# Conditioning parts regrouped over four attention rounds, and one batch routed a round sooner, in an attention and expert kernel

## The reference

```
x = x + attention(cond(x, side, side, w1, u1, time))
x = x + experts(cond(x, side, side, w2, u2, time))
```

## Time and profile before

| | us |
|---|---|
| three runs, median (lowest to highest) | 524.43 (522.4 to 524.53) |
| the profiled execution, its time | 527.21 |
| the profiled execution, its span | 525.4 |
| PE busy in the span | 456.2 (87%) |
| DVE busy | 345.7 (66%) |
| ACT busy | 310.5 (59%) |
| POOL busy | 213.5 (41%) |

### The profile page before, as it was taken

The page is one execution under the profiler, slowest core; times in us unless marked ns, Lnnn a source line. Parts: engine busy times, 40 slices in busy tenths (PEclk is TensorE's granted clock), DMA queues, the critical chain, the costliest instruction groups (busy, mean ns, idle before and its releaser), DMA issues.

```text
span 525.4 us, 10372 instructions
## 1 busy us (share of the span) xinstructions
PE 456.2 (87%) x3073; PEld 343.8 (65%) x3073; DVE 345.7 (66%) x1204; ACT 310.5 (59%) x854; POOL 213.5 (41%) x224
## 2 busy tenths in 40 slices
PE   4487889999999889998998957868999999999476
PEld 1266677787777768786886643446777777777222
DVE  4948769559668678739859883835567777674043
ACT  4366687689585787968798670113436656666200
POOL 0323402006012365111357877403666666666600
PEclk9889899999999999999999977979999999999879
DMA  7931494000030011200029997499855555560297
GB/s 268 418 138 36 87 193 108 20 1 1 0 83 0 30 65 71 78 5 2 21 82 380 406 408 282 116 300 310 276 143 161 157 148 156 166 166 18 55 404 293
DMA packets 47318, 79.49 MB, mean 151 GB/s; under 512 B 8266, under 2 KB 31127, under 8 KB 46880
## 3 DMA queue, kind: packets, MB, share of 16 engines
q1 hardware_dynamic: 36544, 55.08, 33.4%
q0 software_dynamic: 7680, 16.93, 8.9%
q10 hardware_dynamic: 3040, 6.82, 4.0%
HBM read 56.54 MB, written 26.44 MB: 158 GB/s over the span
## 4 chain that ended last, share of the span: by engine, by line
PE 52%; DVE 15%; ACT 14%; DMA 9%; issue 5%; POOL 3%; SPq 2%; DVEq 0%; POOLq 0%; ACTq 0%
PE ps L1698 11%; PE ps L1400 8%; PE ps L1719 7%; PE ps L1525 6%; ACT lg L696 4%; DVE lg L1042 3%; ACT lg L639 3%; DMA pairs<-pair_rows 3%; PE ps L1448 2%; PE ps L1396 2%; POOL slot_rows L618 2%; PE ps L1397 2%; PE ps L1398 2%; DMA xrow<-slot_rows 2%; DMA pair_rows<-eout,dest 2%
## 5 line engine op out<-in xcount | busy, mean ns | idle before, releaser
L625 POOL DMA_INDIRECT pair_rows<-eout,dest x93 | 91.9, 988 | 62.4 <-ACT eout L639 40.4
L696 ACT ACTIVATE lg<-lg,mneg 128x128 f32<-128x128 f32 (+1 forms) x128 | 56.4, 443 | 26.1 <-DVE mneg L1042 26.1
L1698 PE MATMUL ps<-wts,xg 128*64 (+1 forms) x512 | 70.2, 339 | 1.2 <-DVE xg L1319 1.1
L546 POOL DMA_INDIRECT slot_rows<-rows,pair_slot x48 | 48.4, 1009 | 34.6 <-issue 23.6
L1698 PEld LDWEIGHTS ps<-wts,xg 128*64 128x64 f32 x512 | 52.3, 141 | 13.2 <-issue 5.7
L1525 PE MATMUL ps<-oT,wo_sb 128*128 128x256 f32 x240 | 54.4, 380 | 0.0
L1319 DVE COPY xg<-ps 128x512 f32<-128x512 f32 (+1 forms) x50 | 33.4, 667 | 31.0 <-PE ps L1400 28.8
L1525 PEld LDWEIGHTS ps<-oT,wo_sb 128*128 128x128 f32 x240 | 44.6, 190 | 6.2 <-ACT oT L639 0.7
L838 ACT ACTIVATE sact<-ps 128x192 f32<-128x192 f32 (+1 forms) x50 | 16.2, 325 | 51.5 <-PE ps L1698 49.1
L639 ACT ACTIVATE lg<-lg,rinv 128x128 f32<-128x128 f32 (+1 forms) x128 | 45.9, 449 | 0.8 <-DVE rinv L1050 0.8
L1719 PE MATMUL ps<-wts,aT 96*64 96x256 f32 (+1 forms) x256 | 46.0, 379 | 0.4 <-ACT aT L639 0.4
(11 more groups left out here) (237 smaller groups left out, 1199.8 us busy)
## 6 DMA issues: line engine op xcount, KB each, us to landing
wts<-in_experts_dram SPq DMA_DIRECT2D x22, 640.0 KB, 14.0
xrow<-slot_rows SPq DMA_DIRECT2D x188, 65.0 KB
pairs<-pair_rows SPq DMA_DIRECT2D x16, 512.0 KB, 9.6
wts<-in_experts_dram ACTq DMA_DIRECT2D x10, 640.0 KB, 7.9
slot_rows<-zero SPq DMA_DIRECT2D x1, 4160.0 KB, 24.3
wT<-in_wq_t_dram SPq DMA_DIRECT2D x4, 512.0 KB, 6.2
wq_raw<-in_wq_l_dram SPq DMA_DIRECT2D x1, 2048.0 KB, 14.7
wo_sb<-in_wo_l_dram SPq DMA_DIRECT2D x1, 2048.0 KB, 20.6
```

The costliest lines, as they stand in the source:

```text
L546: nc.gpsimd.indirect_dma_start(out=slot_d, out_offset=bass.IndirectOffsetOnAxis(ap=pair_slot[:, t, k:k + 1], axis=0), in_=r[:, k, :], in_o ...
L625: nc.gpsimd.indirect_dma_start(out=pair_d, out_offset=bass.IndirectOffsetOnAxis(ap=dest[:, d:d + 1], axis=0), in_=out_rows(d), in_offset=N ...
L696: ins = nc.scalar.activation(t, t, ACT.Exp, bias=mneg[:, u % 2, c:c + 1], scale=-1.0, accum_out=rsum[:, u % 2, c:c + 1])
L1698: ins = nc.tensor.matmul(ps[h * R:(h + 1) * R, 2 + u % 2, k * I2:(k + 1) * I2], xg[u % len(xg)][:, k, cc, h * R:(h + 1) * R], moving, star ...
```

## The change

Four rounds (5, 6, 10 and 11) do three parts where they did two, the second of the late ones being new; all parts behind come sooner, and rounds 13 and 14 have none. Batch 1 is routed from round 8 on instead of 9, and its two blocks are sent in rounds 10 and 11 instead of 11 and 12. The sends of block 4, which stood in two halves around the last `cond_sums` on POOL, stand together.

```
+        THICK = (5, 6, 10, 11)
+
         def round_parts(u):
-
-            return round_jobs[2 * u:2 * u + 1], round_jobs[2 * u + 1:2 * u + 2]
-
-
-        routed_from = (4, 9, 12)
-        block_round = (6, 7, 11, 12, 13, 14)
+            first = 2 * u + sum(1 for r in THICK if r < u)
+            return round_jobs[first:first + 1], round_jobs[first + 1:first + (3 if u in THICK else 2)]
+
+
+        routed_from = (4, 8, 12)
+        block_round = (6, 7, 10, 11, 13, 14)
...
                         if part == 2:
-                            for t in sent_in(u):
-                                if t == TB * QUICK:
-                                    number_rows(t)
-                                    send_rows(t, range(TOPK // 2))
                             cond_sums((c, jb))
...
                 for t in sent_in(u):
-                    if t == TB * QUICK:
-                        send_rows(t, range(TOPK // 2, TOPK))
-                    else:
-                        number_rows(t)
-                        if t == LAST[0] - 1:
-                            number_last_rows(LAST[1])
-                        send_rows(t, range(TOPK))
+                    number_rows(t)
+                    if t == LAST[0] - 1:
+                        number_last_rows(LAST[1])
+                    send_rows(t, range(TOPK))
```

## The result

The change made the kernel slower: 542.44 us median of four runs (540.51 to 547.41) against 524.48 of before on the same chip (522.4 to 525.1), ratio 1.0356, 95% interval 1.0311 to 1.04. On another chip six more runs gave 540.38 (e9), ratio 1.033 [1.0273, 1.0387]; the median of all ten is 540.8, 16.4 over the 524.4 of before's fifteen. I had forecast 537.3.

A forecast was written before the change was run, and what follows sets the result against it. The prediction took PE, busy 456 of 525 us, and its chain of waits through the attention rounds as the bound. Waits +9.8, port +1.6 and clock +1.5 made +12.9, giving a median of 537.3 us, range 527.5 to 543.

The forecast's parts named there:

- PE idle, rounds 6 to 15, without the added port: PE's waits in rounds 6 to 15, summed round by round: 20.05 us after against 10.3 before, +9.8.
- port, beyond what before had: POOL's additions slow DVE at the pick in round 5 (0.6) and the hits of round 11 (1.0): +1.6 us.
- clock: PE at half clock behind new waits of 5.75 and 4.1 us, most of it at round 6: +1.5 us.
- two stretches of 1.95: Upper limit of the clock cost: 1.95 us twice, behind the new waits of 5.75 and 4.1 us.
- rounds 13 to 15, 1.6 us of idle: Rounds 13 to 15 lose their parts; PE's idle time of 2.75 us becomes about 1.6.
- my 5.75: Round 6: part 2 ahead of the pick makes it 4.06 us later; PE's idle 1.7 becomes 5.75 us.
- upper bound of 5.1: Port: both POOL additions met in full in rounds 5 and 11, 2.55 us each, 5.1 in all.
- the 0.9 for the gate logits: Round 12 with the start of 13: part 3 ahead of the next logits makes route_logits another 0.9 us late.
- A: Rival: only round 6's stall is real, later rounds absorb each other's lateness; +3.7, 528 us; chance 0.19.
- B: Rival: faster through the freed tail, rounds 13 to 15 emptied and round 6's stall shrunk; -4.5, 520 us; chance 0.05.
- C: Rival: evens out within 0.5%, round 6's loss paid by rounds 7 and 14; 525 us; chance 0.08.
- D: Rival: POOL's additions met in full at both places, both stretches at 1.2 GHz; +17.9, 542 us; chance 0.08.

The follow-up runs named there:

- e9: The changed kernel once more, unaltered, on another chip: 540.38 us, ratio 1.033 to before.
- e6: The changed kernel with POOL's two additions held back until the pick of batch 0 (round 5) and the hits of block 3 (round 11) are through: 539.63 us.
- e5: The changed kernel with unread matmuls on PE ahead of two waits, 7 in round 6 and 6 in round 12: 535.3 us, ratio 1.0242 to before.
- e1: The kernel before with single part (0,3,2) moved from the front of round 6 to round 5, ahead of the pick of batch 0: 530.86 us.
- e4: The changed kernel with part (1,3,2) moved from late in round 11 to early in round 12: 535.22 us, ratio 1.0222 to before.
- e10: The changed kernel with picks ahead of the late parts and part (1,3,2) in round 12 instead of 11: 532.75 us, ratio 1.0146 to before.
- e7: The kernel before with part 1 of jobs (0,3) and (1,2) moved from late to early in rounds 5 and 10: 518.38 us, ratio 0.9894.
- e12: The kernel before with the eight sends of block 4 together behind POOL's two additions of job (1,3): 528.72 us, ratio 1.0082.
- e2: The kernel before with the picks of batches 0 and 1 ahead of the late part of their round: 523.93 us, ratio 0.9999.
- e8: The kernel of e7 with ACT's copy hh of batch 3 behind the filled rows of round 7: 519.47 us, ratio 0.9918 to before.
- e3: The changed kernel with the picks of batches 0 and 1 ahead of the late parts of their rounds: 539.07 us, ratio 1.0303 to before.
- e11: The changed kernel with a new table of parts, and ACT's early exponentials and hh behind fill_rows: 531.83 us, ratio 1.0145 to before.

## Why the prediction was wrong in size and right in kind

**The sum.** I forecast +12.9 on the profiled execution and found +13.3, but by accident: the start and the tail gave back 4.2 us of the 17.5 lost in the rounds. The steps, one by one:

| step | forecast | measured |
|---|---|---|
| PE idle, rounds 6 to 15, without the added port | +9.8 | +9.5 |
| port, beyond what before had | +1.6 | +2.6 (e6) |
| clock | +1.5 | +4.8 (after against e5) |
| not assigned | | +0.6 |
| together | +12.9 | +17.5 in the rounds |

The rows say what the lost time consists of, not what each would give back: with POOL's work moved (e6) the waits fell by 3.3 us, rounds 6 and 12 by 1.75.

**The step that failed is "I take +1.5" for the clock.** I bounded it by two stretches of 1.95 and reasoned that PE would be the path in round 6 only. The two stretches cost 3.1, and the third, 1.7, I had not counted at all, because I looked only at the two long waits: round 15's wait of 2.3 us was forecast as part of "rounds 13 to 15, 1.6 us of idle". That the clock falls behind a wait of this length was open from the rows of before, where 1.7 kept it and 3.42 did not; I took the upper row as if it were the limit. The trace of before had more, in round 0, which the prediction did not use: there 0.50 follows a wait of 1.59 us, 3.9 us behind another of 2.72.

```profile
55.31 1.04 PE L1400 MATMUL ps<-ident,lg 128*128 128x128 f32 x4 [1.59 <-DVE mneg L1042]
```

```profile
55.38:58.79 3.41, 3.41 (x17) 3.41 (x18) 3.38 (x2) 0.60 (x1) 2.90 (x3) 0.50 0.00 0
```

**The port** was taken at 1.6 over what before had. e6 shows 3.3 in the two waits; of the 1.7 in round 6 about 0.7 was in my 5.75 already, since the pick of before also ran beside POOL, beside its masks (0.59 below and 0.81 in the earlier trace rows against 0.23 and 0.48 in e6), so that the added part is 1.0 and 1.6, 2.6 in all, half of the upper bound of 5.1. DVE, then POOL, in before:

```profile
156.86 0.59 DVE L1075 TENSOR_SCALAR picked<-rrep 128x128 f32<-128x128 f32 x1
```

```profile
156.73 1.22 POOL L519 TENSOR_SCALAR_AFFINE_SELECT bm<-bm 128x512 f32<-128x512 f32 x2 [10.24 <-DMA bm<-bias_rows]
```

The wait of round 12 has the rest, in two hits of block 3 in the changed kernel:

```profile
270.80 0.91 DVE L1102 SCALAR_TENSOR_TENSOR hit<-key,ktop,rcomb 128x64 f32<-128x64 f32 x1
...
271.64 1.29 DVE L1102 SCALAR_TENSOR_TENSOR hit<-key,ktop,rcomb 128x64 f32<-128x64 f32 x1
...
272.87 0.28 DVE L1102 SCALAR_TENSOR_TENSOR hit<-key,ktop,rcomb 128x64 f32<-128x64 f32 x1
```

The first two end at 271.71 and 272.93, with POOL's two additions (271.63 and 272.85), and in e6 a `rsum` of four columns, 0.16 us elsewhere, took 1.11 until one of them ended. So DVE's operation ended only with POOL's. This agrees with the rule of the Trainium skill (SBUF — State Buffer, Who interferes with whom), that the later one is held for the other's length. The sum stayed under the bound because each pair of additions began beside operations that went on at their usual lengths: 0.7 us in round 5, beside the `MAX8` and the replacements of the pick, 0.4 in round 11, beside the addition to x. The time of the held operation itself passes inside the wait, too.

**Waits, place by place** (forecast, measured): round 6 5.75 and 0.6 of port, 6.7; round 7 with the start of 8 0.95, 0.8; round 8 1.25, 1.8; round 9 0.2, none; round 10 1.3, 1.3; round 11 2.5, 2.5; round 12 with the start of 13 6.5 and 1.0 of port, 6.9; rounds 13 to 15 1.6, 2.3. ACT's wait of 3.65 for `hf` went. The ledger made by hand from the order and the durations was right within 1 us at every place (in round 12 the 0.9 for the gate logits, counted in the 6.5, did not come, and the wait ahead of scores(14) was 5.5 where I had 4.1 and the port). The part 3 that stands behind the `ql` there is that of the same job (1,3), not of a next one. Runs e1, e4 and e10 show that the stalls of rounds 6 and 12 are independent.

**The median.** I took the 2.8 us between before's profiled execution and its median off the forecast. Its rounds began at 52.3 us, the latest start of fourteen, which is as much as the difference, but it is not shown to be the cause: the profiled executions of e7 and e12 were 2.8 and 2.6 over their medians with starts at 49.6 and 49.3. Subtracting was right by its outcome; 537.3 fell short of the 540.8 of all ten runs by 3.5, about the 3.3 missing from the clock term.

**Rivals.** A fell: the later rounds absorb nothing (e1), and round 12 stalls by itself (e4). B fell: the emptied rounds 13 and 14 gave 1.0 us (rounds 13 and 14 together 21.1 against 22.2), and round 15 at the lower clock took back more, 1.7. C fell. D named the result, 542, with both stretches cold; it had the port in full in place of the third stretch, so that its number is nearer than its mechanism. The range 527.5 to 543 held the first median, 542.44, at its very end, and the ratio put on the median before, 543.1, lies outside it: its upper end stood 1 us above D's forecast and left no room for D itself to come out higher.

**Open.** Behind the rounds the profiles of before, e2, e7 and e8 take 222.5 to 224.4 us, and those of the changed kernel, of e9 and of its variants e3 to e6 220.8 to 222.0; but e1, a variant of before, takes 222.0, and e10 and e11, variants of the changed kernel, 223.1 and 224.1, so that this may be chance; it was not tried. Nor is it known what decides whether the clock falls behind a wait of about 2 us. The smaller waits (rounds 8, 10 and 11) are read from the trace and were not removed one by one.

## What to carry to other kernels

On an in-order engine a piece of work costs what stands behind it and is waited for, so it belongs where the engine idles ahead of no consumer: one more part behind the logits of round 5 cost 7 us (e1), and the part that stood there won time when it went some 8 us forward, to where DVE idled (e7), while reordering within a full stretch moved the wait only (e2). The stall of e1 was not caught up in nine later rounds, since there every engine waits for another, and a stall can bring two followers that should be priced with it: the clock, as a chance, for every wait as long as the shortest behind which any trace shows it down (here 1.6 us), and the work that the moved piece releases on another engine at the same moment. Moving several places at once hides a good idea behind bad neighbours; try each cut alone.

## What the runs showed of the hardware

- The granted clock fell to 0.50 behind waits of about 2 us in some executions and not in others. The wait of 1.8 us in round 8 of the changed kernel left the clock at 1.00 in the profiles of after, e4, e5 and e9, and round 8 lasted 17.7 us; in e3, e6 and e10 the round lasted 19.4, 21.0 and 19.4. The wait of 2.3 ahead of round 15 was followed by 0.50 in after, e6 and e9 and by 1.00 in e3 and e5; one of 1.95 in its place by 0.50 in e11 and by 1.00 in e4 and e10. The wait of 1.59 in round 0 was followed by 0.50 in nine of the twelve profiles that have it, all but e3, e4 and e5, and round 0 then lasted 19.3 us instead of 17.8. The runs of the changed kernel spread more than those of before: 537.6 to 547.4 us over ten, with mean clocks of 0.955 to 0.937, where before had 521.9 to 527.9 over eleven beside e9.
- The start of the rounds varies by 4 us between executions whatever the kernel, which is more than most of the effects studied here; two profiles are better compared from a common point just ahead of the first difference (here round 6) than by their spans, for round 0 itself lasts between 16.5 and 19.3 us.
